# Experts in short code with one batch up front, a router stage with rings of four, and a feed-forward stage over 14 tiles of 128 tokens

## The reference, cut to what matters

```python
x = x + L0_xattn(layernorm(x), ctx, ctx, ...)   # 16 heads of 16, softmax over 375 context rows
x = x + L0_ffn(layernorm(x), ...)               # router and 32 experts (below)
x = x + L1_xattn(layernorm(x), ctx, ctx, ...)   # as L0, scores negated
x = x + L1_ffn(layernorm(x), ...)               # fp4 feed-forward (below)

# L0_ffn: 40 scores a token (32 experts, 8 that only scale x), the best 6 by score + bias count
scores = softmax(x @ classifier.T);  _, idx = top_k(scores + bias, 6)
for each of 32 experts:  out += w_e * (silu(x @ Wgate_e.T) * (x @ Wup_e.T)) @ Wdown_e.T   # inner width 128
# L1_ffn: inner width 704; x, h and all weights are rounded in blocks of 16 to the fp4 grid
h = silu(fp4(x) @ fp4(w_gate).T) * (fp4(x) @ fp4(w_up).T);  out = fp4(h) @ fp4(w_down).T
```

## Time and profile before

| | |
|---|---|
| median of 3 runs | 1039.37 us |
| the profiled execution, its own time | 1036.13 us |
| its span, mean granted clock | 1034.4 us, 0.958 |
| busy: PE, DVE, ACT, POOL | 921.6, 672.1, 409.0, 275.6 us |
| 0 to 100 us | keys and queries of layer 0 |
| 100 to 306 us | attention of layer 0 |
| 306 to 388 us | router stage |
| 388 to 608 us | experts |
| 608 to 860 us | attention of layer 1 with its front |
| 860 to 1034 us | feed-forward |

### The profile page before, as it was taken

How to read it: one execution, slowest core, us unless ns; L and a number is a source line. 1 busy time by engine, 2 the same in 40 slices (tenths; PEclk the granted TensorE clock), 3 DMA queues, 4 the chain that set the end, 5 groups by cost and what they waited for, 6 DMA issues and landing times.

```text
span 1034.4 us, 20395 instructions
## 1 busy us (share of the span) xinstructions
PE 921.6 (89%) x7334; PEld 711.4 (69%) x7334; DVE 672.1 (65%) x1410; ACT 409.0 (40%) x934; POOL 275.6 (27%) x289
## 2 busy tenths in 40 slices
PE   2996899999989779999998967899999997898897
PEld 1773787788857348898897843578888874555554
DVE  4455677878844925455554464577777745999995
ACT  1342566666646551111111112466666663121221
POOL 8012676666661440000000004000000001444442
PEclk9998899999996999999999987999999989999999
DMA  9689444544131657212103213255554200000000
GB/s 281 185 240 206 90 92 90 104 97 93 37 92 45 207 179 151 65 31 64 32 16 111 65 49 60 58 108 97 101 95 90 62 2 0 5 13 9 13 13 18
DMA packets 102847, 87.07 MB, mean 84 GB/s; under 512 B 43618, under 2 KB 94178, under 8 KB 102626
## 3 DMA queue, kind: packets, MB, share of 16 engines
q1 hardware_dynamic: 102738, 85.58, 34.5%
HBM read 67.52 MB, written 17.79 MB: 82 GB/s over the span
## 4 chain that ended last, share of the span: by engine, by line
PE 61%; DVE 15%; issue 10%; DMA 6%; POOL 3%; SPq 2%; ACT 1%; DVEq 0%; POOLq 0%; ACTq 0%
PE ps L901 12%; PE ps L785 8%; PE ps L731 8%; PE ps L717 7%; PE ps L745 7%; PE ps L908 7%; PE ps L635 3%; DVE Pr L1272 2%; PE ps L794 2%; DMA Qz<-mT 2%; DMA wgu<-wgu 2%; DVE Pr L1277 2%; DVE Pr L1275 2%; PE ps L705 2%; DVE amh L1529 1%
## 5 line engine op out<-in xcount | busy, mean ns | idle before, releaser
L1335 DVE TENSOR_REDUCE ext<-ps 112x2 f32<-112x750 f32 x256 | 232.6, 933 | 57.4 <-PE ps L717 54.2
L1097 ACT ACTIVATE Pr<-ps 125x448 f32<-125x448 f32 x384 | 199.1, 543 | 87.7 <-PE ps L731 74.3
L901 PE MATMUL ps<-xT,wgu 128*128 128x224 f32 x704 | 149.2, 354 | 12.9 <-issue 4.9
L901 PEld LDWEIGHTS ps<-xT,wgu 128*128 128x128 f32 x704 | 132.1, 190 | 23.4 <-issue 11.4
L731 PE MATMUL ps<-Qz,Kp 98*125 98x224 f16 x768 | 131.2, 266 | 11.4 <-DMA Qz<-mT 9.2
L717 PE MATMUL ps<-Kp,Qz 96*112 96x375 f16 x512 | 121.1, 329 | 5.1 <-DMA Qz<-qscr 4.2
L731 PEld LDWEIGHTS ps<-Qz,Kp 98*125 98x125 f16 x768 | 95.0, 138 | 44.4 <-DMA Qz<-mT 13.2
L785 PE MATMUL ps<-wv,ctx 128*125 128x256 f32 x384 | 119.2, 396 | 2.4 <-ACT Vx L1103 1.2
L635 PE MATMUL ps<-ctx,wk 128*128 128x375 f32 x256 | 96.4, 526 | 23.9 <-DMA bqk<-bqk 14.2
L1467 DVE TENSOR_TENSOR Pr<-Pr,ps 128x224 f32<-128x224 f32 x88 | 34.2, 388 | 123.1 <-ACT Pr L1169 65.0
L528 POOL TENSOR_TENSOR X<-X,bo 112x256 f32 x32 | 22.6, 725 | 295.8 <-DVE Pr L1253 243.7
(11 more groups left out here) (151 smaller groups left out, 1183.9 us busy)
## 6 DMA issues: line engine op xcount, KB each, us to landing
ctx<-ctxT SPq DMA_DIRECT2D x64, 375.0 KB, 3.7
Kp<-kscr SPq DMA_DIRECT2D x96, 187.5 KB, 4.9
kscr<-ksp SPq DMA_DIRECT2D x32, 375.0 KB, 3.7
wgu<-wgu SPq DMA_DIRECT2D x32, 256.0 KB, 2.8
Qz<-qscr SPq DMA_DIRECT2D x174, 28.0 KB, 4.1
wdn<-wdn SPq DMA_DIRECT2D x32, 128.0 KB, 3.0
X<-x_in SPq DMA_DIRECT2D x1, 1792.0 KB, 11.6
qscr<-qsp SPq DMA_DIRECT2D x16, 112.0 KB, 4.3
```

Of the source, the lines that this page charges most:

```text
L901: last = mm(ps[:, bank, half_ * CT:(half_ + 1) * CT], wgu_sb[e % NE][:, q, EI * half_:EI * half_ + EI], xT2[:, q, c * CT:(c + 1) * CT], st ...
L1097: A(Pr[g % 2][0:KC, j, GI * t:GI * t + GI, :].rearrange("r h q -> r (h q)"), ps[0:KC, 4 + k % 2, 0:GI * S], ACT.Exp, scale=scale).then_inc ...
L1335: V.tensor_reduce(ext[0:S, 2 * p:2 * p + 2], ps[0:S, 2 * (p % 2):2 * (p % 2) + 2, 0:M], AX_X, red).then_inc(row_maximum_taken, 1)
```

## The change

**Keys of layer 1.** The rings for context (kctx) and split keys (nksp) have four places, the further ones in space that attention has left. Keys 0 and 1 are projected inside the tail of attention of layer 0, key 2 behind its last product; ACT's three key passes come ahead of the router's copies, key 3's behind them. The full-width copy kfull keeps two places and PSUM two from key 4 on. The mask sum on PE now stands behind key 14.

**Router.** One copy a batch on ACT, into xT2; the loops are unrolled.

**Experts.** Only batch 0 is computed for all experts. The 15 other batches are 3 turns of 5 batches in two parts of 3 and 2, in a hardware loop on PE, for experts that batches 1 to 15 use. The first part of each expert stands in the code once, ahead of the If. Weights come in one DMA an expert into a ring of 11, of which seven places lie in the two Pr buffers.

**Feed-forward.** After each residual add of layer 1, SP stores the batch to DRAM (xscr) and loads back tiles of 128 tokens; statistics are taken per tile. The stage runs over 14 tiles on 128 partitions. The clamp step leaves DVE for ACT, as two passes (Relu, then Identity); the subtraction of MAGIC leaves DVE for POOL, ahead of x_back and h_back.

```diff
-CH = 8
-CB = B // CH
-CT = CB * S
+CT = 2 * S
+TURN = 5
+TURNS_OF = (B - 1) // TURN
+PARTS = ((0, 3), (3, 2))
+R = 128
+T = B * S // R
+LAST_OF = [(R * t + R - 1) // S for t in range(T)]
-NE = 4
+NE, NO, NP = 11, 4, 2
+NK = 4
...
+                def relay(b):
+                    if b >= 3:
+                        sp.wait_ge(x_stored, 16 * (b - 2))
+                        if b - 3 in LAST_OF:
+                            t = LAST_OF.index(b - 3)
+                            wait_from(sp, tile_loaded, 16 * t)
+                            sp.dma_start(XT[:, t * D:(t + 1) * D], xscr[t * R:(t + 1) * R, :]).then_inc(tile_loaded, 16)
+                    if 2 <= b < B + 2:
+                        sp.wait_ge(residual_added, B + b - 1)
+                        sp.dma_start(xscr[(b - 2) * S:(b - 1) * S, :], X[:, (b - 2) * D:(b - 1) * D]).then_inc(x_stored, 16)
...
+                    if l == 1:
+                        relay(b)
                     flatten(b + 1)
...
+                    for n in range(B + 1):
+                        if n + NK < B:
+                            sp.wait_ge(keys_projected, B + n + 2)
+                            load_keys_ctx(n + NK)
+                        if n > 0:
+                            store_next_keys(n - 1)
...
             def x_back(i, par):
                 pool.wait_ge(x_rounded, i + 1)
+                G.tensor_tensor(qrx, qrx, qcx, ALU.subtract).then_inc(x_less_magic, 1)
+                pool.wait_ge(x_less_magic, i + 1)
...
             def h_back(i, par):
                 pool.wait_ge(h_rounded, i + 1)
+                G.tensor_tensor(qrh, qrh, qch, ALU.subtract).then_inc(h_less_magic, 1)
+                pool.wait_ge(h_less_magic, i + 1)
...
                 turn_sums(g0 + B - 1)
+                if l == 0:
+                    project_next_keys(0)
                 turn_values(g0 + B - 1)
+                if l == 0:
+                    project_next_keys(1)
                 project_out(g0 + B - 1)
...
-                    pe.wait_ge(residual_added, B)
-                    pe.wait_ge(values_normalised, B)
-                    after = 16 * (B // 2 + 1)
-                    for par in (0, 1):
-                        project_keys(1, B + par, par, after)
+                    project_next_keys(2)
...
+                    for n in range(3, B - 1):
+                        project_next_keys(n)
                     pe.wait_ge(used_by_token, 1)
-                    pe.wait_ge(experts_xT_copied, B + 2)
                     mm(ps[0:1, 2, 0:ER], onecol[0:S, :], used[0:S, :], start=True, stop=True).then_inc(used_by_chunks, 1)
+                    project_next_keys(B - 1)
...
                     for e in range(ER):
+                        first_gate_up(e + 1)
+                        first_down(e)
                         with pe.If(in_rest(e)):
-                            for c in range(1, CH):
-                                rest_gate_up(e, c)
-                                if c == 1:
-                                    first_down(e)
-                                else:
-                                    rest_down(e, c - 1)
-                            first_gate_up(e + 1)
-                            rest_down(e, CH - 1)
-                        with pe.Else():
-                            first_gate_up(e + 1)
-                            first_down(e)
+                            with pe.Fori(0, TURNS_OF) as i:
+                                for k, (b0, nb) in enumerate(PARTS):
+                                    if k == 1:
+                                        pe.wait_ge(first_gated, min(e + 2, ER))
+                                    gate_up(e, bass.ds(i * (TURN * S) + (b0 + 1) * S, nb * S), *rest_at(k), rest_gate_up_ready)
+                                rest_down(e, 0)
+                                pe.wait_ge(first_added, e + 1)
+                                rest_down(e, 1)
...
+            def h_magic(i):                       # ScalarE; x_magic is the same on qcx
+                act.wait_ge(h_exponents_ready, i + 1)
+                A(qch, qch, ACT.Relu, bias=magic[:, 0:1], scale=MAGIC).then_inc(h_steps_cut, 1)
+                act.wait_ge(h_steps_cut, i + 1)
+                A(qch, qch, ACT.Identity, bias=magic[:, 1:2]).then_inc(h_magic_ready, 1)
+            def ffn_batch(i, first=False, left=2):
+                if left >= 2:
+                    x_magic(i + 2)
+                h_magic(i)
+                if left >= 1:
+                    gate(i + 1)
+                if not first:
+                    h_turned(i - 1)
+                if left >= 2:
+                    xq_turned(i + 2)
...
-                    ch.link(V.tensor_reduce(used[0:S, :], W[0:S, CB * ET:].rearrange("q (b e) -> q e b", e=ET)[:, 0:ER, :],
+                    ch.link(V.tensor_reduce(used[0:S, :], W[0:S, ET:].rearrange("q (b e) -> q e b", e=ET)[:, 0:ER, :],
...
+            def ffn_batch(i, par, left=3, sums=True):     # VectorE
                 if left >= 2:
-                    x_fp4(i + 2)
+                    x_exponents(i + 2)
+                if sums:
+                    ffn_sum(i - 2)
+                h_exponents(i)
                 if left >= 3:
                     x_scales(i + 3, 1 - par)
-                dve.wait_ge(h_divided, i + 1)
-                to_fp4(S, qrh, qch, FI).then_inc(h_rounded, 1)
+                if left >= 2:
+                    x_round(i + 2)
+                h_round(i)
                 if left >= 1:
                     gate_h(i + 1, 1 - par)
-                if not start:
-                    ffn_sum(i - 1)
```

More of the change, by code:

```diff
@@ L904, in gate_up, with down @@
                         last.then_inc(done, 1)
-                    def down(e, h, bank, done):
-                        for v in range(CB):
-                            last = mm(ps[0:S, bank, v * D:(v + 1) * D], h[:, v * S:(v + 1) * S], wdn_sb[e % NE][:, :],
-                                      start=True, stop=True)
+                    def down(e, h, outs, done):
+                        for v, out in enumerate(outs):
+                            last = mm(out, h[:, v * S:(v + 1) * S], expert_sb[e % NE][:, 2 * C2 * EI:], start=True, stop=True)
@@ L936, in rest_down @@
                         pe.wait_ge(rest_added, n)
-                        down(e, hrest[c % 2], 6 + c % 2, rest_down_ready)
+                        down(e, hrest[k], [rest_sum(k, v) for v in range(PARTS[k][1])], rest_down_ready)
                     first_gate_up(0)
@@ L1036, in keys_high @@
                 act.wait_ge(split_stored[par], i * (32 - 16 * l) + (32 * (B // 2 * l) + 16))
-                if l == 1:
-                    act.wait_ge(keys_low_ready, g)
-                    for m in range(C2):
-                        A(kfull[par][:, m, :], ps[:, 4 + 2 * par + m, 0:M], ACT.Identity, bias=bqk[1][:, 2 + m:3 + m])
                 for m in range(C2):
@@ L1208, in _ @@
+            x_magic(0)
             xq_turned(0)
+            x_magic(1)
             gate(0)
             xq_turned(1)
-            gate(1)
-            xq_turned(2)
-            with act.Fori(0, B - 3) as i:
-                gate(i + 2)
-                h_turned(i)
-                xq_turned(i + 3)
-            gate(B - 1)
-            for i in range(B - 3, B):
-                h_turned(i)
+            ffn_batch(0, first=True)
+            with act.Fori(0, T - 3) as i:
+                ffn_batch(i + 1)
@@ new lines, in exponents, with add_magic, x_exponents, x_round @@
+            def exponents(r, c, done):
+                V.tensor_scalar(c.bitcast(U32), r.bitcast(U32), 0x7F800000, None, ALU.bitwise_and).then_inc(done, 1)
+            def add_magic(r, c, done):
+                V.scalar_tensor_tensor(r, r, PRED, c, ALU.mult, ALU.add).then_inc(done, 1)
+            def x_exponents(i):
+                dve.wait_ge(x_divided, i + 1)
+                exponents(qrx, qcx, x_exponents_ready)
+            def x_round(i):
+                dve.wait_ge(x_magic_ready, i + 1)
+                add_magic(qrx, qcx, x_rounded)
@@ L1575, in _ @@
-            norms(True)
+            FIRST = T - 2
+            for t in range(FIRST):
+                if LAST_OF[t] > B - 5:
+                    tile_stats(t)
+            tile_norms(0, FIRST)
             x_scales(0, 0)
-            x_fp4(0)
+            x_exponents(0)
+            x_round(0)
             x_scales(1, 1)
-            x_fp4(1)
+            x_exponents(1)
+            x_round(1)
             x_scales(2, 0)
             gate_h(0, 0)
-            ffn_batch(0, 0, start=True)
-            with dve.Fori(0, (B - 4) // 2) as i:
-                ch.enter(i, 2 * (2 + 3 + 3 + 3))
-                ffn_batch(i * 2 + 1, 1)
-                ffn_batch(i * 2 + 2, 0)
@@ L1587, in _ @@
-            ch.leave((B - 4) // 2)
-            ffn_batch(B - 3, 1, left=2)
-            ffn_batch(B - 2, 0, left=1)
-            ffn_batch(B - 1, 1, left=0)
-            ffn_sum(B - 1)
+            ffn_batch(0, 0, sums=False)
```

(8 more changed lines are left out.)

435 lines of the change are left out of this document (259 added, 176 removed).

## The result

The changed kernel takes 1002.28 us (median of 4, 999.17 to 1005.61) against 1039.7 us; the ratio is 0.9638, 95% interval 0.9574 to 0.9701: 37 us faster.

The account below looks back on a forecast made before the run. PE held 61% of the chain; DVE bound the feed-forward. Router -10.1, experts -11.2, attention 0, feed-forward -6 sum to -27.3 from 1036.1: 1008.8, or 1012 as that execution was 3.2 below the median; own range 1003 to 1022, with rivals 997 to 1026.

Parts of the forecast that it names:

- rival B: Feed-forward: DVE and POOL interleave without loss; 9.4 us a tile, -20 us instead of -6, 998 us; chance 0.2.
- a tile at 9.6 or less: Feed-forward: tile time named ahead as showing the forecast wrong, with DVE and POOL interleaving without loss.
- Keys 0 to 2: Attention 0's tail: projections delay the last residual add by 3 us (0 to 5); router copies start near 315 again.
- Nothing is lost: Router start: the add's delay costs nothing, since keys and ACT's passes already held the first copy until 315.20.
- Keys 3 to 14: Router stage: twelve keys at 2.5 us, +1.3 for half clock, +1.8 for DMA; 33.1 us, ending at 364.4.
- rival C: Router stage: keys keep their pace of 3.7 us, 44.4 us instead of 33.1; +11, 1023 us; chance 0.12.
- DVE's chain: Router stage: 4 us late start, +6 for POOL collisions; first expert gate at 378.3 instead of 388.35, -10.1 us.
- Experts: Expert stage: 27 turns of 5.9 us, 32 first parts of 1.40 us; 208.8 against 220 us, -11.2.
- Attention 1: Attention of layer 1: fewer statistics on DVE, extra SP DMAs; 0 us, between -1 and +3.
- Feed-forward: Feed-forward stage: 14 tiles of 10.4 us, -8.6; start +1, end +2, one statistic less; -6 us.
- Exclusion: DVE operations with two SBUF inputs and POOL operations block each other; without it a tile would take about 9.4 us.
- D: Experts: code fetch holds skipped experts at 3.46 us; 47 us more, less the 4 taken, 1055 us; chance 0.05.

Follow-up runs that it names:

- e7: Changed kernel, but ACT may begin the passes of key n only when key n-2 is stored, not n-4; 1010.43 us, ratio 0.9707.
- e6: Changed kernel with the router's exponential ahead of ACT's passes over key 3; 1001.98 us, ratio 0.9617.
- e10: Changed kernel with the router's exponential ahead of ACT's passes over key 3 and PE's mask sum ahead of key 14; 1000.28 us, ratio 0.9661.
- e8: Changed kernel with expert 10's bit cleared in the mask, so eight experts are computed over the rest instead of nine; 986.32 us, ratio 0.9470.
- e1: Changed kernel with all four feed-forward rounding steps back on DVE, no clamp on ACT or subtraction on POOL; 996.55 us, ratio 0.9593.
- e2: Changed kernel with only the two feed-forward subtractions back on DVE, the clamping passes staying on ACT; 996.23 us, ratio 0.9598.

## Why the prediction was right, and where its sizes were off

The mechanisms held, with the sign of each stage for which one was forecast and the sum (-27.3 predicted, -30.6 between the spans, -37.4 between the medians). Two things were luck. The errors of the feed-forward cancelled, as told below; and 1002.28 us lies below the forecast's own 1003 to 1022, inside the stated range only because that was opened for rival B. Of the signs named ahead, the first gate, the turns, POOL's busy time and its stretched operation came; the tile of 10.2 to 10.7 us and a DVE under 7 us a tile did not (9.54 and 7.8), and "a tile at 9.6 or less" had been named as the sign for B. By its steps:

- **Keys 0 to 2.** The add came 3.8 us late (predicted 3). "Nothing is lost" was wrong by 2.4 us: the copies began at 317.64, not 315, since they waited for the late add and for norms that took 6.4 us from the end of the add to the first normalised batch, where before has 4.6 (one of their operations stretched from 0.17 to 1.57 behind POOL, row 314.20). With that key 3 began at 334.2, not 331.3.
- **Keys 3 to 14.** 33.1 us predicted, 31.9 measured; the 1.8 for the DMA did not come, and rival C (the keys keep their pace) was e7's kernel, at +9.8.
- **DVE's chain.** The exponential came 4 us late and the chain from its sum to the mask input took 26.8 us where the earlier trace rows have 21.4: +5.4. Eight of its operations are stretched, by 9.9 us in all, where before has four, by 4.3; the prediction counted five before and priced five more at 6. Gate at 379.15 for 378.3. What the step missed is that its own 4 us could be had back (e6, e10).
- **Experts.** 27 turns of 5.93 (5.9), 32 first parts of 1.31 (1.40; its 0.093 us is what one of the eight products would stream), 5.5 us for start and stalls (4.5 in the same places). Nine rest experts, and the ninth's 17.7 us are e8's 18.4. The stage of before was 222.2 us rather than 220, the rest of the difference.
- **Attention 1.** Predicted 0, +2.5 between the two profiles; in all the profiles of this study that have its code it took 249.1 to 254.7 us. What moves it stays open; none of the runs was made for it.
- **Feed-forward, the term mis-sized.** The middle: 10.4 us predicted, 9.54 measured. From the end of h_over (913.18) to the x subtraction 2.19, as predicted (0.46 + 1.35 + 0.36). Then POOL's six operations take 6.43 for 6.66, the stretch of x_back (0.45) not counted; h_round holds POOL up for 0.60 where 0.96 was reckoned, and why it is so little is not shown; the handoffs are 0.32 for 0.6: the 0.9. The ends: start +1 predicted, +3.0 measured; end +2, +3.0; and the 4.8 us of two long periods not seen at all. That the errors cancelled to 3 us was luck. The stage of before had 16 batches of 9.64; e1, with DVE's old steps, shows that the 14 tiles (with the new order on DVE, which no run parts from them) bring 17.0 us, and that the moved rounding then costs 7.8 of them. That the move would be no gain was in the prediction; that its cost sits at the ends was not.
- **Exclusion.** The same expression costs 1.24 us for 0.89 when a POOL operation is in its way (row 915.60), and e2 against the changed kernel prices the subtraction on POOL at 0.95 us a tile or more. DVE's operations with one input wait as well (1.12 us for 0.26, groups above), which is why DVE is busy 7.8 us a tile and not under 7. The Trainium skill (SBUF — State Buffer, Who interferes with whom) has the two engines share one port pair under an exclusive lock; the traces agree for the operations with two SBUF inputs. By that rule the clamp on ACT is free of it, and the traces agree: from 881 us on ACT's passes over x take 0.51 us in all ten tiles, though they run beside h_over on POOL.
- **Rivals.** B (9.4 us a tile, -20) had the period nearly right and for the wrong reason: the subtraction takes 1.68 us, not 1.39, and the exclusion is there; its stage was 11 us off. C did not come (keys 2.5 us apart); D never showed: skipped experts run every 1.31 us.

## What to carry to other kernels

When steps move between engines, judge each by itself (here one was worth 1.15 us a tile and the other cost 0.95, at least), and price the first and last round apart from the middle: a step that hides in a full pipeline is bare there, and a wait removed at the end can come back as a gap elsewhere. A small operation that stands behind a long one in its engine's queue (the exponential behind a key, the mask sum behind a key) costs the whole item in front of it; move it before making anything faster.
